# The dense feed-forward head runs inside the next attention chunk, and the membrane recurrence runs on GpSimd

## The reference, cut to what matters

```python
h = silu(causal_conv(rms(x)))                        # 4 taps
q, k, v = norm(h @ wq), norm(h @ wk), h @ wv
sd, ab = h @ w_spike, silu(h @ w_au + b_au) @ w_ad + b_ad
for t in range(256):                                 # 8 heads, s is 64 x 128
    mem = 0.9 * mem + sd[t]                          # the membrane
    hard = mem > 0.5
    mem = mem - hard * 0.5
    alpha, beta = sigmoid(ab[t] + alpha_spike * hard), sigmoid(bb[t] + sum(hard * beta_spike))
    s = s * alpha
    s = s - beta * outer(k[t], k[t] @ s) + beta * outer(k[t], v[t])
    y[t] = q[t] @ s
# the dense head: per token, no recurrence
gate = sigmoid(silu(x @ w_u1 + b_u1) @ w_u2 + b_u2)
y = x + (rms(y) * w_hn) @ w_out * gate
y = y + (silu(rms(y) @ w_ff1) * (rms(y) @ w_ff3)) @ w_ff2
xl = layernorm(x + y)
# routing and experts
aff = xl @ centroids.T; e = argmax(aff)              # one of 8 experts a token
z = xl + sigmoid(aff[e]) * (relu(w1[e] @ ln(xl) + b1[e]) @ w2[e] + b2[e])
out = layernorm(xl + z)
```

## Time and profile before

| | |
|---|---|
| timed runs, median | 2171.9 us |
| the profiled execution | 2175.1 us, of which the span is 2173.4 |
| PE (TensorE) busy | 1553.1 us, 71% |
| DVE (VectorE) busy | 1274.1 us, 59% |
| ACT (ScalarE) busy | 612.4 us, 28% |
| POOL (GpSimd) busy | 368.1 us, 17% |
| mean granted clock of PE | 0.84 of full speed |

### The profile page before, as it was taken

How to read it: one execution, slowest core, us unless ns; L and a number is a source line. 1 busy time by engine, 2 the same in 40 slices (tenths; PEclk the granted TensorE clock), 3 DMA queues, 4 the chain that set the end, 5 groups by cost and what they waited for, 6 DMA issues and landing times. The chain is left out here.

```text
span 2173.4 us, 43513 instructions
## 1 busy us (share of the span) xinstructions
PE 1553.1 (71%) x16904; PEld 955.8 (44%) x16904; DVE 1274.1 (59%) x3384; ACT 612.4 (28%) x1224; POOL 368.1 (17%) x513
## 2 busy tenths in 40 slices
PE   1248977887797788778778878877894676564551
PEld 0023654464365446435543643554362353334551
DVE  1748656865865685586567558655552545454445
ACT  2041234124123412422341242133022323332221
POOL 2110131013012201301220130032010112111005
PEclk9577987997898799789979987997896867778995
DMA  1351101100110010011001001100104000001112
GB/s 52 121 189 30 31 11 31 22 9 12 30 31 7 26 30 12 12 30 28 9 17 39 11 12 30 26 6 12 44 11 139 15 15 28 16 10 31 37 32 80
DMA packets 160304, 72.63 MB, mean 33 GB/s; under 512 B 129505, under 2 KB 141089, under 8 KB 160098
## 3 DMA queue, kind: packets, MB, share of 16 engines
q1 hardware_dynamic: 148962, 46.66, 8.6%
q10 hardware_dynamic: 8448, 16.78, 2.1%
q0 software_dynamic: 2688, 6.30, 1.0%
HBM read 31.49 MB, written 38.21 MB: 32 GB/s over the span
## 5 line engine op out<-in xcount | busy, mean ns | idle before, releaser
L455 POOL COPY kx<-kend_t 32x256 f32<-32x256 f32 x256 | 114.5, 447 | 896.3 <-PE ps L909 853.7
L855 PE MATMUL ps<-wv,ident 128*128 128x512 f32 x480 | 231.1, 631 | 37.3 <-DVEq L1208 37.2
L1267 DVE SCALAR_TENSOR_TENSOR state<-state,gam,ps 128x128 f32<-128x128 f32 x512 | 137.5, 341 | 74.2 <-PE ps L909 74.2
L855 PEld LDWEIGHTS ps<-wv,ident 128*128 128x128 f32 x480 | 92.1, 199 | 174.7 <-issue 153.4
L1223 DVE TENSOR_TENSOR nv<-ps,nrm 128x512 f32<-128x512 f32 x64 | 44.2, 691 | 209.6 <-PE ps L797 209.0
L1090 DVE TENSOR_TENSOR kq_leaf<-kq,eleaf 128x1024 f32<-128x1024 f32 x32 | 40.4, 1264 | 156.5 <-ACT dleaf L562 107.2
L909 PE MATMUL ps<-w,kx 128*64 128x128 f32 x2048 | 128.8, 280 | 0.0
L909 PEld LDWEIGHTS ps<-w,kx 128*64 128x64 f32 x2048 | 113.4, 139 | 13.0 <-issue 13.0
L1195 DVE TENSOR_TENSOR tmp<-kq,kq_blk 128x31 f32<-128x31 f32 (+15 forms) x248 | 114.5, 462 | 1.3
L813 PE MATMUL ps<-yt,wout 128*128 128x128 f32 x512 | 89.2, 346 | 26.4 <-ACT yt L542 26.4
L720 PE MATMUL ps<-yt,headind 128*16 128x512 f32 x128 | 85.9, 809 | 29.9 <-ACT yt L535 29.9
(11 more groups left out here) (268 smaller groups left out, 3273.8 us busy)
## 6 DMA issues: line engine op xcount, KB each, us to landing
slot_d<-zeros ACTq DMA_DIRECT2D x16, 1024.0 KB, 13.1
b_d<-ab SPq DMA_DIRECT2D x32, 128.0 KB, 2.0
a_d<-kq_pair SPq DMA_DIRECT2D x8, 512.0 KB, 2.6
kq_blk<-a_d SPq DMA_DIRECT2D x32, 128.0 KB, 2.9
u_d<-kq SPq DMA_DIRECT2D x8, 512.0 KB, 2.6
ub<-u_d SPq DMA_DIRECT2D x128, 32.0 KB, 1.9
bb<-b_d SPq DMA_DIRECT2D x128, 32.0 KB, 1.9
wall<-in_w SPq DMA_DIRECT2D x8, 512.0 KB, 7.3
```

The lines of the kernel that those rows point to most:

```text
L455: m = pool.tensor_copy(kx[part, :, b4, :], kend_t[part, g, 2 * q:2 * q + 2, :])
L855: pe.matmul(bd[k % 2].t[:, :], ident[:, :], wv[:, 0:512], start=True, stop=True)
L1267: k = dve.scalar_tensor_tensor(out=state[:, hp, b, :], in0=state[:, hp, b, :], scalar=gam[:, hp, b:b + 1], in1=bd[j].t[:, DV * x:DV * x + ...
```

## The change

- **Head.** A class `Head` keeps the head's weights and routing state in SBUF through both blocks, and `head_on_tensor`, `head_on_scalar`, `head_on_vector`, `head_on_pool` and `head_on_sync` hold its stages. Chunk c-1's head runs in body(c): DVE's stages inside the solve and the routing in the state loop, PE's at the pace points, ACT's ahead of and behind the copies of `sd`, GpSimd's scatter at the body's end. `feed_forward` keeps the last chunk's head alone; the normed rows `xl` and the routing's `meta` of every chunk go to DRAM and come back for the tail (`places` at half of the expert tiles). `attn` stays in SBUF.
- **Membrane.** GpSimd does it, in three instructions a step, split before and after the head's `xsum`. It is time-scaled: the inputs are multiplied by 0.9^-(t+1) (`pace_t`), ahead of the `sd` products, so that the recurrence has no decay factor; DVE's `decays(0)` scales the carry back and compares with `pace_t` for the spikes, and waits for `mem_done`.
- **PE.** `KEEP_WARM` goes from 3 to 2 and writes to another bank; `predict(0)` stands behind the next chunk's tokens; `bb` and `b_d` are gone, and the product for `y` takes 32x32 blocks of `ab`, sixteen matmuls a tile for four.

```diff
-KEEP_WARM = 3
+KEEP_WARM = 2
...
+def head_on_vector(dve, c, w, stage, settle=lambda: None):
+    if stage == "y1":
+        dve.wait_ge(w.b.drained.sem, w.b.emptied(c, "u2"))
+        dve.scalar_tensor_tensor(out=w.gate, in0=w.gate, scalar=1.0, in1=hd.attn[:, :], op0=ALU.add,
+                                 op1=ALU.mult).then_inc(hd.gated.sem, 1)
+        dve.wait_ge(hd.gated.sem, hd.gated.at(c, 1))
+        dve.scalar_tensor_tensor(out=w.y1, in0=w.gate, scalar=0.5, in1=w.x, op0=ALU.mult,
+                                 op1=ALU.add).then_inc(hd.y1_ready.sem, 1)
+    if stage == "h2":
+        dve.wait_ge(hd.rs_ready.sem, hd.rs_ready.at(c, 1))
+        dve.scalar_tensor_tensor(out=w.h2, in0=w.y1, scalar=hd.wffn[:, 0:1], in1=w.rs, op0=ALU.mult,
+                                 op1=ALU.mult).then_inc(hd.h2_ready.sem, 1)
...
+def head_on_pool(pool, c, w, stage, settle=lambda: None):
+    if stage == "xsum":
+        pool.wait_ge(hd.y1_ready.sem, hd.y1_ready.at(c, 1))
+        pool.tensor_tensor(w.xsum, w.y1, w.x, ALU.add).then_inc(hd.xsum_ready.sem, 1)
+    if stage == "scatter":
+        pool.wait_ge(hd.slot_ready.sem, hd.slot_ready.at(c, 1))
+        pool.wait_ge(hd.xh_ready.sem, hd.xh_ready.at(c, 1))
+        for g in range(NG):
+            pool.indirect_dma_start(hd.slot_d, bass.IndirectOffsetOnAxis(hd.slot[:, g:g + 1], 0), w.xh[:, g, :],
+                                    None).then_inc(hd.scattered.sem, 16)
...
+        def membrane(f, steps):
+            for t in steps:
+                if t == 0:
+                    for p in range(HP):
+                        b = bank_of[f"sd{p}"]
+                        pool.wait_ge(b.drained.sem, b.emptied(f, f"sd{p}"))
+                    settle(f)
+                now = mem[:, :, :, t]
+                last = carry[:, :].rearrange("p (a b) -> p a b", b=NB) if t == 0 else mem[:, :, :, t - 1]
+                level = DECAY ** -t
+                if t:
+                    pool.wait_ge(rec_step, 3 * t)
+                pool.tensor_scalar(residue[:, :].rearrange("p (a b) -> p a b", b=NB), last, level, -level,
+                                   ALU.is_gt, ALU.mult).then_inc(rec_step, 1)
+                pool.tensor_tensor(now, now, last, ALU.add).then_inc(rec_step, 1)
+                pool.wait_ge(rec_step, 3 * t + 2)
+                i = pool.tensor_tensor(now, now, residue[:, :].rearrange("p (a b) -> p a b", b=NB), ALU.add)
+                i.then_inc(rec_step if t < CH - 1 else mem_done.sem, 1)
...
             pool.memset(tu, 0.0).then_inc(tu_cleared.sem, 1)
+            if nxt:
+                driven(nxt)
+                membrane(nxt, range(0, CH // 2))
+            if before(last):
+                pool.wait_ge(hd.scattered.sem, hd.scattered.at(before(last), 16 * NG))
+            if last:
+                head_on_pool(pool, last, room, "xsum", lambda: settle(c))
+            if nxt:
+                membrane(nxt, range(CH // 2, CH))
...
+            if last:
+                act.wait_ge(kend_ready.sem, kend_ready.at(c, HP))
+                head_on_scalar(act, last, room, "tu")
+            if nxt:
+                drives(nxt)
+            if last:
+                head_on_scalar(act, last, room, "gate")
                 load_exp_log_table(nc, act)
+                head_on_scalar(act, last, room, "rs")
+                for t in range(FT):
+                    head_on_scalar(act, last, room, t)
+                load_exp_log_table(nc, act)
+                for stage in ("rstd0", "xt", "rstd1"):
+                    head_on_scalar(act, last, room, stage)
+            elif nxt:
+                load_exp_log_table(nc, act)
+            if nxt:
                 decays(nxt, 0)
...
-            predict(c, 0, runs)
+            for j in range(2):
+                pe.wait_ge(bd[j].drained.sem, bd[j].freed(c, "d0"))
+            if last:
+                head_on_tensor(pe, last, room, "u1", lambda: settle(c))
             if nxt:
                 tokens(nxt)
-            for j in range(2):
-                pe.wait_ge(bd[j].drained.sem, bd[j].freed(c, "d0"))
+            predict(c, 0, runs)
+            pe.wait_ge(by.drained.sem, by.freed(c, "y0"))
+            pe.wait_ge(bw.drained.sem, bw.freed(c, "w0"))
+            stages = {0: "u2", 2: "ms", 3: 0, 4: 1, 5: 2, 6: 3, 7: "ff", 8: "xt", 9: "aff"}
             for n in range(PACES):
                 pe.wait_ge(pace.sem, pace.at(c, n + 1))
                 settle(c)
+                if last and n in stages:
+                    head_on_tensor(pe, last, room, stages[n], lambda: settle(c))
                 for k in range(KEEP_WARM):
-                    pe.matmul(bd[k % 2].t[:, :], ident[:, :], wv[:, 0:512], start=True, stop=True)
+                    pe.matmul(bw.t[:, :], ident[:, :], wv[:, 0:512], start=True, stop=True)
...
                     for hq in range(4):
-                        cols = slice(DV * hq, DV * hq + DV)
-                        m = pe.matmul(by.t[:, cols], bb[:, g % 2, 4 * q + hq, :], w[:, hq, :], start=(hq == 0),
-                                      stop=False)
+                        hp, h2, cols = 2 * q + hq // 2, hq % 2, slice(DV * hq, DV * hq + DV)
+                        for b4 in range(GB):
+                            part = slice(CH * b4, CH * b4 + CH)
+                            m = pe.matmul(by.t[part, cols], ab[part, hp, 1, 2 * g + h2, :], w[part, hq, :],
+                                          start=(hq == 0), stop=False)
...
-                dve.wait_ge(rec_step, 2 * CH)
-                dve.sem_clear(rec_step)
-                dve.tensor_copy(carry[:, :], mem[:, :, :, CH - 1].rearrange("p a b -> p (a b)"))
-                dve.tensor_scalar(sp[:, :, :].rearrange("p a n -> p (a n)"),
-                                  mem[:, :, :, :].rearrange("p a b t -> p (a b t)"), THR2, None,
+                dve.wait_ge(mem_done.sem, mem_done.at(f, 1))
+                dve.tensor_scalar(carry[:, :], mem[:, :, :, CH - 1].rearrange("p a b -> p (a b)"), DECAY ** CH, None,
+                                  ALU.mult)
+                dve.tensor_tensor(sp[:, :, :].rearrange("p a (b t) -> p (a b) t", t=CH),
+                                  mem[:, :, :, :].rearrange("p a b t -> p (a b) t"),
+                                  pace_t[:, :].unsqueeze(1).broadcast_to([P, HP * NB, CH]),
                                   ALU.is_gt).then_inc(sp_ready.sem, 1)
...
-        def solve(c, other):
-            rest = [n for n in range(2 * CH)] if other else []
+        def solve(c, last):
+            stages = {0: "y1", 5: "h2", 8: 0, 11: 1, 15: 2, 19: 3, 25: "stat0", 27: "xl", 28: "stat1", 30: "xh"}
             dve.sem_inc(pace.sem, 2)
+            if last:
+                dve.wait_ge(kend_ready.sem, kend_ready.at(c, HP))
+                b = bank_of[f"kend{HP - 1}"]
+                dve.wait_ge(b.full.sem, b.filled(c, f"kend{HP - 1}"))
+                head_on_vector(dve, last, room, "zu")
+                head_on_vector(dve, last, room, "u1")
             dve.wait_ge(na_loaded.sem, na_loaded.at(c, 64))
             dve.wait_ge(tu_cleared.sem, tu_cleared.at(c, 1))
             diag = lambda t: t.rearrange("p i j -> p (i j)")[:, 0:CH * CH:CH + 1]
@@ -1195,19 +1605,13 @@
                 dve.tensor_tensor(prod, tu[:, 0:n, j:j + 1].broadcast_to([P, n, m]),
                                   na[:, j + 1:CH, j].unsqueeze(1).broadcast_to([P, n, m]),
                                   ALU.mult).then_inc(tri_step, 1)
-                if other and j == 0:
-                    driven(other)
-                if rest:
-                    membrane(rest.pop(0))
                 dve.wait_ge(tri_step, 2 * j + 2)
                 i = dve.tensor_tensor(tu[:, 0:n, j + 1:CH], tu[:, 0:n, j + 1:CH], prod, ALU.subtract)
                 i.then_inc(tri_step if j < CH - 2 else tri_done.sem, 1)
-                if rest:
-                    membrane(rest.pop(0))
                 if j % 4 == 0:
                     dve.sem_inc(pace.sem, 1)
-            for n in rest:
-                membrane(n)
+                if last and j in stages:
+                    head_on_vector(dve, last, room, stages[j], lambda: settle(c))
...
+        routing = {1: "pick", 2: "sums", 3: "gates", 6: "slots"}
...
-            solve(c, nxt)
+            solve(c, last)
             values(c, 0)
+            if last:
+                head_on_vector(dve, last, room, "aff")
             if nxt:
...
+                if last and i in routing:
+                    head_on_vector(dve, last, room, routing[i])
...
+        for stage in ("u1", "u2", "ms", 0, 1, 2, 3, "ff", "xt", "aff"):
+            head_on_tensor(pe, end, room, stage)
+        pe.wait_ge(s_experts, n_experts)
+        for e in range(E):
+            for t in range(FT):
+                m = pe.matmul(bcount.t[:, FT * e + t:FT * e + t + 1], wall[:, e, P * t:P * t + P], lnb[:, e:e + 1],
+                              start=True, stop=True)
+        m.then_inc(s_b1, 1)
```

(41 more changed lines are left out.)

849 lines of the change are left out of this document (392 added, 457 removed).

## The result

The changed kernel takes 2111.6 us (median of 4 runs, 2105.7 to 2123.3), the kernel before 2173.7 in the same comparison: ratio 0.972, 95% interval 0.967 to 0.977. The forecast was 2149. The direction came out and the time lies in the range, but 62 us were gained where 23 were forecast: terms of the sum were wrong. The profiled execution took 2105.7 us (span 2104.0) and is compared with the span of 2173.4 before.

What follows compares the result with a forecast made beforehand. It read the kernel by stages: DVE bounds the solve, PE the state loop, hand-overs the separate head phase. Head phase -251, attention chunks +226, tail +2 gave -23 us, so 2149 us for the median, range 2080 to 2235.

Steps and rivals of the forecast that it cites:

- Meetings of DVE and GpSimd, 0.2 us each: In the solve: each instruction meeting a GpSimd membrane instruction is 0.2 us later; 55 meetings, 11 us, in chunks 1 to 6.
- the sum: Whole kernel: all terms added, -251 + 226 + 2 = -23 us, median 2149; as a case, chance 0.40, range 2115 to 2185.
- Its other sign, DVE's largest wait for `mem_done`: On DVE: the mechanism would be wrong if its largest wait were for the membrane's end on GpSimd; no size given.
- GpSimd's step at 0.95 us: Membrane on GpSimd: one step alone takes 0.95 us, 30.4 us a chunk; +11.6 us ahead of chunk 0, including `sp`.
- The head inside the solve: Solve of chunks 1 to 6: y1 holds DVE 3.7 us, head with hand-overs 12, other waits 0.9.
- Chunk 0: First chunk, whole membrane but no head: solve +7.7, DVE's decays wait +10.7, with +1.7 and the clock +22 us.
- Loop and clock: State loop, each chunk: blocks for the y product +1.7, rank +0.5, PE's clock +2.0 us.
- The head phase: End of attention to the expert tiles: only the last chunk's head stays, 65.7 us, saving 251 us.
- B: Solve beside GpSimd: the engines hardly disturb each other, or GpSimd's small instructions are near 0.15 us; about 2060; chance 0.2.
- C: Behind the solve: membrane ends later, DVE's decays wait for `mem_done`, once a step exceeds 1.7 us; about 2250; chance 0.2.
- D: State loop on PE: the 32x32 products for y don't overlap, +147 us, about 2295; chance 0.06.
- E: Solve: head not really hidden, 3 to 4 us a chunk more waits; within 10 us of 2172; chance 0.14.

Runs made afterwards that it cites:

- experiment 2: The changed kernel with time steps 1 to 30 of the membrane left out (6 of 96 GpSimd instructions stay): 2039.1 us, ratio 0.937.
- experiment 4: The changed kernel, membrane replaced by 36 GpSimd instructions of 128x512 or 96 of 128x128 a chunk: 2224.6 and 2154.8 us, one execution each.
- experiment 1: The changed kernel with the membrane back on DVE, between the solve's instructions, everything else as changed: 2083.7 us, ratio 0.960.
- experiment 5: KEEP_WARM at 3 instead of 2 in the changed kernel: 2146.9 us (0.986); at 2 instead of 3 in the kernel before: 2203.0 us (1.012).
- experiments 5 and 6: Experiment 5 has its own line; 6 is the kernel before with only the y product in 32x32 blocks: 2216.9 us; also with KEEP_WARM 2: 2220.8 us.

## Why the prediction was wrong

- *Meetings of DVE and GpSimd, 0.2 us each: wrong, and the step that failed.* It made 11 us a solve in six chunks and 12.4 in chunk 0; the runs show 1.7 (experiment 2 against the changed kernel) and 2.1 (29.35 us against 27.24 bare). That is 56 and 10 us too many, 66 of the sum. It came from instructions of 512 columns and was applied to instructions of 64 as a price per meeting; experiment 4 shows 0.56 us at 512 columns and 0.02 at 64. By the prediction's own sign ("if the solve's instructions aren't stretched") its mechanism fails: a product takes 549 ns for 465, a subtraction 373 for 389, where 200 more a meeting were expected. Its other sign, DVE's largest wait for `mem_done`, is half there: the longest single waits are those for the membrane (47 us ahead of chunk 0, 18 in it), in a steady chunk the longest are on PE (8.5) as before.
- *GpSimd's step at 0.95 us: too low*, 1.35 measured alone and 1.55 beside the solve. It is 13 of the 16 us that are missing ahead of chunk 0 (the other 3 stay with the membrane on DVE, experiment 1), it makes the membrane end 5 us behind the solve, and the wait, six times 2.5, is 15 of the extra 17 us before `r`. With chunk 0's 9 that makes some 37 us, and it worked against the first error. That the time stayed in the range is luck: without this error it would be near 2075 by these numbers, below 2080.
- *The head inside the solve: right in sum*, 16.6 against 16.9 us. In its parts y1 waits 2.3 us and not 3.7 (mean of six in experiment 2), and the rest is 14.6 for 12.9. In chunk 7, without GpSimd and y1's wait, 13.1 against 12.9.
- *Chunk 0:* forecast +7.7 in the solve and +10.7 behind it; measured -2.6 (29.35 for 31.96) and +19.3 to the first `r`, of which 18.1 are the wait for the membrane.
- *Loop and clock:* forecast 4.2 us a chunk in the loop, of which 2.2 for blocks and rank and 2.0 for the clock; measured 2.3. Where the clock is at 1.00 (experiment 1) the loop takes 68.1 us in the mean for 68.4 before, so blocks and rank cost nothing, and the 2.7 more in the changed kernel go with its lower clock. In chunk 7 the loop is 5.9 us *shorter* (64.8 at a clock of 1.00 for 70.7 at 0.93), which is most of why that chunk costs 8.8 and not 16. The key phase is 1.8 us a chunk shorter, where nothing was forecast. That these small terms nearly cancel is partly luck: experiments 5 and 6 show single parts of the change moving the total by 27 to 40 us, mostly through stages that they don't touch.
- *The head phase:* 67.8 for 65.7 us; *tail:* +5.0 for +2, within what it varies by (experiment 5).
- *Rivals.* B had the mechanism (hardly any disturbance) and 2060, and C its place (DVE waits for `mem_done`) at 2.5 us a chunk. That wait came at 1.55 us a step, below C's 1.7, because the solve beside it was 9 us shorter than forecast; the time lies between B and the sum. D is refuted by the 1.07 us row. E forecast a wash and is refuted by the 2.8%. None of them asked what a faster kernel than the changed one would be, the head moved and the membrane left on DVE. The numbers for that stood in the prediction: 31.9 against 27.2 us of solve make 4.7 us for the membrane on DVE.

Not settled: what sets the length of the key phase, and what decides where in it the clock falls. Both differ between kernels whose work there is the same, and no edit tried here held the clock up at a gain. Why the gather and store at the end take 42 or 49 us is open too. Whether `bb` by DMA would be better than blocks in the changed kernel wasn't tried.

## What to carry to other kernels

A price read from one pair of long instructions is not the price of short ones: scale it down to the size in question, or measure it at that size. A slow recurrence on an idle engine needs a long stage beside it, so cost it beside the stage as it will be, and price each of two moves alone as well: here one of them by itself beats both. A stage that exists once with nothing to hide it, such as the first chunk, may want the faster engine. Before a difference of 1 or 2% between variants is explained by their code, compare a stage that neither touches: here such stages changed as well, by as much as 7 us at the end and 4 us a chunk in the key phase.

## What the runs showed of the hardware

- GpSimd takes 0.32 to 0.36 us for a two-input instruction of 128x64 and 0.48 for one with two operations on one input, where two inputs of 128x512 take 1.04: far above an eighth. A dependent step of the three takes 1.35.
- DVE's 64 membrane instructions of 0.27 us cost a full solve 4.7 to 5.0 us, not 17: they lie in the gaps between instructions that depend on each other (31.9 for 27.2 us before; 49.2 for 44.2 with the head).
- Thirty-two products of 32x32 blocks take 1.07 us on PE at a clock of 1.00, less than eight of 128x128 (1.16).
- One warming product more a pace point made one kernel 35 us slower, and one less made its parent 27 us slower, mostly in stages that hold none of them: the key phase in the first (24 us of it), the state loop (12), the tail (7) and the key phase (6) in the second.
